# Logarithm and exponential in place of square root and reciprocal, powers on GpSimd, activation tables loaded ahead

## What is computed

```python
def _layernorm(x, axis=-1, eps=1e-05):
    m = jnp.mean(x, axis=axis, keepdims=True)
    v = jnp.var(x, axis=axis, keepdims=True)
    return (x - m) / jnp.sqrt(v + eps)

def l2norm(t):
    return t / jnp.clip(jnp.linalg.norm(t, axis=-1, keepdims=True), 1e-12)
```

## Time and profile before

| | us |
|---|---|
| Median of three runs | 2251.84 (2251.66 to 2254.59) |
| The profiled execution | 2245.9 |
| Its span in the profile | 2244.0 |
| Granted TensorE clock, mean | 0.971 |
| TensorE busy | 2001.5 |
| VectorE busy | 1459.5 |
| ScalarE busy | 1171.3 |
| GpSimd busy | 812.8 |

### The profile page before, as it was taken

One profiled execution on the slowest core, in us unless ns is written; L12 is line 12 of the kernel. 1 busy time (PEld: TensorE's weight loads), 2 busy tenths in 40 slices (PEclk: granted clock), 3 DMA queues, 4 the chain that ended last, 5 costly groups with the idle time before them and its releaser, 6 DMA issues.

```text
span 2244.0 us, 44998 instructions
## 1 busy us (share of the span) xinstructions
PE 2001.5 (89%) x17759; PEld 1185.9 (53%) x17759; DVE 1459.5 (65%) x2920; ACT 1171.3 (52%) x1950; POOL 812.8 (36%) x1153
## 2 busy tenths in 40 slices
PE   6887789988978999998998898999799899999888
PEld 3333456666644454544665444445465666666546
DVE  6775688878778777764555875121677676767474
ACT  2575456666613454565332567332576675757432
POOL 4554434333137847442001421000545344453042
PEclk9999999999989999999999999999999999999999
DMA  3430111111234424211101320000565564655161
GB/s 126 149 101 2 30 30 30 27 32 28 84 90 125 143 81 137 75 34 58 48 1 63 98 79 11 32 0 6 167 206 180 168 208 127 208 178 168 49 130 42
DMA packets 183993, 199.15 MB, mean 89 GB/s; under 512 B 55922, under 2 KB 152486, under 8 KB 179302
## 3 DMA queue, kind: packets, MB, share of 16 engines
q1 hardware_dynamic: 183782, 196.27, 29.8%
HBM read 93.53 MB, written 92.08 MB: 83 GB/s over the span
## 4 chain that ended last, share of the span: by engine, by line
PE 35%; DVE 6%; ACT 6%; issue 3%; DMA 2%; POOL 2%; SPq 1%; DVEq 0%; ACTq 0%; POOLq 0%
PE PS L2149 5%; PE PS L359 4%; PE PS L2398 3%; PE PS L2414 3%; PE PS L2386 3%; PE PS L2000 3%; ACT AR L2558 3%; PE PS L1987 2%; PE PS L1990 2%; PE PS L2752 2%; PE PS L627 1%; PE PS L2740 1%; PE PS L2742 1%; PE PS L606 1%; PE PS L2158 1%
## 5 line engine op out<-in xcount | busy, mean ns | idle before, releaser
L1314 ACT ACTIVATE AR<-PS 128x1024 f32<-128x1024 f32 x160 | 162.6, 1024 | 121.7 <-PE PS L1063 120.7
L749 ACT ACTIVATE AR<-PS 128x1024 f32<-128x1024 f32 x160 | 162.8, 1024 | 91.5 <-PE PS L606 44.9
L1167 DVE TENSOR_REDUCE AR<-PS 128x2 f32<-128x768 f32 (+1 forms) x192 | 159.9, 864 | 50.2 <-PE PS L1042 27.9
L2614 POOL TENSOR_TENSOR RA<-AR,RA 128x288 f32<-128x288 f32 x128 | 88.1, 698 | 276.8 <-DVE RA L2490 143.0
L2558 ACT ACTIVATE AR<-PS,AR 128x512 f32<-128x512 f32 x256 | 174.0, 687 | 25.6 <-DVE AR L2479 25.3
L2479 DVE TENSOR_REDUCE AR<-PS 128x2 f32<-128x1024 f32 x128 | 156.8, 1225 | 12.9
L2386 PE MATMUL PS<-AR 64*128 64x200 f32 (+2 forms) x1280 | 146.9, 354 | 3.0 <-ACT AR L2558 3.0
L1871 POOL TENSOR_TENSOR AR<-AR 128x1024 f32<-128x1024 f32 x32 | 75.5, 2358 | 173.3 <-DVE AR L1722 173.3
L2398 PEld LDWEIGHTS PS<-CC,AR 64*128 64x128 f32 x2048 | 77.9, 140 | 100.4 <-issue 78.0
L2398 PE MATMUL PS<-CC,AR 64*128 64x64 f32 x2048 | 92.4, 229 | 40.9 <-ACT AR L2542 12.4
L2386 PEld LDWEIGHTS PS<-AR 64*128 64x128 f32 x1280 | 111.1, 193 | 6.6 <-ACT AR L2558 3.2
(11 more groups left out here) (371 smaller groups left out, 5027.4 us busy)
## 6 DMA issues: line engine op xcount, KB each, us to landing
ZD<-RC SPq DMA_DIRECT2D x32, 1152.0 KB
AR<-ZD SPq DMA_DIRECT2D x32, 640.0 KB
ZP<-AR SPq DMA_DIRECT2D x128, 160.0 KB, 2.7
SP<-AR SPq DMA_DIRECT2D x40, 384.0 KB, 2.6
AR<-SP SPq DMA_DIRECT2D x128, 96.0 KB
RA<-SP SPq DMA_DIRECT2D x32, 384.0 KB
SP<-AR SPq DMA_DIRECT2D x40, 256.0 KB, 2.9
RC<-RC SPq DMA_DIRECT2D x64, 130.0 KB
```

Source lines behind the costliest of these rows:

```text
L749: e.activation(self.PT[m % 6], C.PS[:, 2 * s:2 * s + 2, :], ACT.Exp).then_inc(S["s_turned"].sem, 1)
L1167: i = e.tensor_reduce(nm[:, :, 4 * up + q:4 * up + q + 1], src[:, :, a:a + wd], AX, ALU.max, negate=True)
L1314: e.activation(self.PT[m % 6], C.PS[:, 2 * s:2 * s + 2, :], ACT.Exp).then_inc(S["s_turned"].sem, 1)
```

## The change

- Every layernorm of `Paired`, `Local`, `Shifted`, `Clipped` and `Routed`: ScalarE computes the logarithm of variance plus epsilon, waits for it on its own semaphore, and then the exponential of -0.5 times it; the reciprocal on VectorE goes, and the result is read from `ST[:, 36:40]`.
- The l2 norm of `Local`: VectorE takes the maximum with 1e-24 right behind the sums, ScalarE a logarithm and an exponential with -0.5; the reciprocal and the multiplication by 8 go from VectorE, and the 8 is in the tables `rqa` and `rqb` that the queries are multiplied with. GpSimd waits for ScalarE in place of VectorE.
- In `Experts` and `Ternary` the root goes from ScalarE to GpSimd, as a power with exponent -0.5 of 128 x 4 numbers; the exponent is a number that VectorE writes in `Begin`. "fin" becomes a step of GpSimd's and none of ScalarE's. In `Ternary` the step "gated" is called "hidden".
- Each stage has `tables`, the set that each of its kinds of steps on ScalarE needs. ScalarE preloads the first one at the start, and after each such step the next one's set if it is another. So a load stands right behind the last activation of the old set and ahead of the copies that follow it.

```diff
@@ -57,7 +57,7 @@
     tile = lambda a: a.reshape(4, 128, 64).transpose(1, 0, 2).reshape(128, 256).astype(f)
-    c["rqa"], c["rqb"], c["rka"], c["rkb"] = tile(ca * s2), tile(sa * s2), tile(ca / s2), tile(sa / s2)
+    c["rqa"], c["rqb"], c["rka"], c["rkb"] = 8 * tile(ca * s2), 8 * tile(sa * s2), tile(ca / s2), tile(sa / s2)
 
@@ -340,17 +340,23 @@
     e.tensor_scalar_add(st[:, 32:36], st[:, 25:32:2], 1e-5).then_inc(vs.sem, 1)
     w.wait_ge(ss, *key)
-    e.reciprocal(st[:, 40:44], st[:, 36:40]).then_inc(vs.sem, 1)
-    w.wait_ge(vs, *key, part=at + 4)
     for q in range(NT):
         i = e.tensor_scalar(dst[:, 128 * q:128 * q + 128], y[:, 128 * q:128 * q + 128],
-                            st[:, 24 + 2 * q:25 + 2 * q], st[:, 40 + q:41 + q], ALU.subtract, ALU.mult)
+                            st[:, 24 + 2 * q:25 + 2 * q], st[:, 36 + q:37 + q], ALU.subtract, ALU.mult)
     i.then_inc(vs.sem, 1)
 
 
 def normalise_scalar(e, w, vs, ss, key, st):
-    w.wait_ge(vs, *key, part=vs.per - 2)
-    e.activation(st[:, 36:40], st[:, 32:36], ACT.Sqrt).then_inc(ss.sem, 1)
+    w.wait_ge(vs, *key, part=vs.per - 1)
+    e.activation(st[:, 40:44], st[:, 32:36], ACT.Ln).then_inc(ss.sem, 1)
+    w.wait_ge(ss, *key, part=1)
+    e.activation(st[:, 36:40], st[:, 40:44], ACT.Exp, scale=-0.5).then_inc(ss.sem, 1)
+
+
+def normalise_gpsimd(e, C, w, vs, gs, key, st):
+    w.wait_ge(C.half)
+    w.wait_ge(vs, *key, part=vs.per - 1)
+    e.tensor_tensor(st[:, 36:40], st[:, 32:36], C.ST[:, 0, 44:45].broadcast_to((128, 4)), ALU.pow).then_inc(gs.sem, 1)
 
 
@@ -374,9 +380,13 @@
 
+EXPS, SILU, GELU, SIGM = "natural_log_exp_and_others", "silu_and_others", "gelu_and_others", "sigmoid_and_others"
+
+
 class Begin:
 
 
+    tables = {"exp": EXPS}
     head, tail, past, sent = 0, NB - 1, None, ("pad",)
@@ -386,6 +396,7 @@
         self.load = {n: C.flag("load_" + n, [()], 96 if n in ("b", "c", "rc") else 16) for n in ("x", "cc", "cb", "a", "b", "c", "rb", "rc", "rd")}
+        C.half = self.S["v_pad"]
         C.load = self.load
@@ -397,6 +408,7 @@
         if step[0] == "pad":
+            e.memset(C.ST[:, 0, 44:45], -0.5)
             e.memset(C.XT[:, :, 512:516], 0.0).then_inc(S["v_pad"].sem, 1)
@@ -427,6 +439,7 @@
 
+    tables = {"turned": EXPS, "fin": EXPS}
     FILLED = {0: {("scores", 0): 40, ("turned", 10): 11, ("turned", 25): 4, ("turned", 70): 5, ("turnx", 2): 8, ("turnx", 3): 12},
@@ -880,6 +893,7 @@
 
+    tables = {"turned": EXPS, "first": EXPS, "ln": EXPS}
     FILLED = {("turned", 40): 11, ("turned", 80): 5}
@@ -1215,11 +1229,9 @@
             w.wait_ge(S["s_ln"], b)
-            e.reciprocal(st[:, 40:44], st[:, 36:40]).then_inc(S["v_fin"].sem, 1)
-            w.wait_ge(S["v_fin"], b, part=1)
             for q in range(NT):
                 i = e.tensor_scalar(dst[:, 128 * q:128 * q + 128], y[:, 128 * q:128 * q + 128],
-                                    st[:, 24 + 2 * q:25 + 2 * q], st[:, 40 + q:41 + q], ALU.subtract, ALU.mult)
+                                    st[:, 24 + 2 * q:25 + 2 * q], st[:, 36 + q:37 + q], ALU.subtract, ALU.mult)
             i.then_inc(S["v_fin"].sem, 1)
@@ -1330,7 +1342,9 @@
             w.wait_ge(S["v_ln"], b)
-            e.activation(st[:, 36:40], st[:, 32:36], ACT.Sqrt).then_inc(S["s_ln"].sem, 1)
+            e.activation(st[:, 40:44], st[:, 32:36], ACT.Ln).then_inc(S["s_ln"].sem, 1)
+            w.wait_ge(S["s_ln"], b, part=1)
+            e.activation(st[:, 36:40], st[:, 40:44], ACT.Exp, scale=-0.5).then_inc(S["s_ln"].sem, 1)
         elif kind == "turnx":
@@ -1444,6 +1458,7 @@
 
+    tables = {"norm": EXPS, "exp": EXPS, "ln": EXPS, "fin": EXPS, "hg": GELU}
     FILLED = {("lin", 0, 0): 11, ("v", 0): 11, ("turnq", 0): 20, ("turnq", 8): 8, ("fill", 27): 10, ("fill", 31): 14, ("ot", 30): 8,
@@ -1727,13 +1742,9 @@
             L = n
-            SM, vn = self.SM[L % 3], S["v_norm"]
-            w.wait_ge(S["s_norm"], L)
-            e.tensor_scalar(SM[:, :, 0:16], SM[:, :, 0:16], 1e-12, None, ALU.max).then_inc(vn.sem, 1)
-            w.wait_ge(vn, L, part=1)
-            e.reciprocal(SM[:, :, 16:32], SM[:, :, 0:16]).then_inc(vn.sem, 1)
-            w.wait_ge(vn, L, part=2)
-            e.tensor_scalar(SM[:, :, 16:24], SM[:, :, 16:24], 8.0, None, ALU.mult).then_inc(vn.sem, 1)
+            SM = self.SM[L % 3]
+            w.wait_ge(S["v_sum"], 4 * L + 3)
+            e.tensor_scalar(SM[:, :, 0:16], SM[:, :, 0:16], 1e-24, None, ALU.max).then_inc(S["v_norm"].sem, 1)
         elif kind == "turnk":
@@ -1823,8 +1834,10 @@
             SM = self.SM[n % 3]
-            w.wait_ge(S["v_sum"], 4 * n + 3)
-            e.activation(SM[:, :, 0:16], SM[:, :, 0:16], ACT.Sqrt).then_inc(S["s_norm"].sem, 1)
+            w.wait_ge(S["v_norm"], n)
+            e.activation(SM[:, :, 0:16], SM[:, :, 0:16], ACT.Ln).then_inc(S["s_norm"].sem, 1)
+            w.wait_ge(S["s_norm"], n, part=1)
+            e.activation(SM[:, :, 16:32], SM[:, :, 0:16], ACT.Exp, scale=-0.5).then_inc(S["s_norm"].sem, 1)
         elif kind == "turnq":
@@ -1871,7 +1884,7 @@
             k3 = kq.rearrange("p (h d) -> p h d", h=16)
-            w.wait_ge(S["v_norm"], n // 4)
+            w.wait_ge(S["s_norm"], n // 4)
             w.wait_ge(S["g_sum"], n)
@@ -1921,6 +1934,7 @@
 
+    tables = {"gate2": EXPS, "hidden": SILU}
     head, tail, past, sent = 0, 0, None, ()
@@ -2069,7 +2084,7 @@
             w.wait_ge(S["v_outward"], 8 * b + 7)
-            normalise_vector(e, w, S["v_fin"], S["s_fin"], key, C.YB[:, b % 2, :], C.ST[:, b % 2, :], C.XK[:, b, :])
+            normalise_vector(e, w, S["v_fin"], S["g_fin"], key, C.YB[:, b % 2, :], C.ST[:, b % 2, :], C.XK[:, b, :])
 
@@ -2083,18 +2098,20 @@
             e.activation(self.SL[n % 3], C.bank[2 * (n % 2)], ACT.Silu).then_inc(S["s_hidden"].sem, 1)
-        elif kind == "fin":
-            b, = key
-            normalise_scalar(e, w, S["v_fin"], S["s_fin"], key, C.ST[:, b % 2, :])
         elif kind == "turnx":
             b, = key
             w.wait_ge(S["t_turnx"], b)
             e.activation(C.XT[:, b, 0:512], C.bank[7], ACT.Copy).then_inc(S["s_turnx"].sem, 1)
 
+    def on_gpsimd(self, e, w, step):
+        C, S, key = self.C, self.S, step[1:]
+        normalise_gpsimd(e, C, w, S["v_fin"], S["g_fin"], key, C.ST[:, key[0] % 2, :])
+
 
 class Ternary:
 
 
+    tables = {"hidden": SILU, "inner": GELU}
     head, tail, past, sent = 0, 0, None, ()
...
@@ -2222,6 +2241,7 @@
 
+    tables = {"exp": EXPS, "fin": EXPS}
     head, tail, past, sent = 0, 0, None, ("lay", "skew", "band", "gather", "send", "rep")
@@ -2661,6 +2681,7 @@
 
+    tables = {"gate1": SIGM, "hidden": SILU, "fin": EXPS}
     head, tail, past, sent = 0, 0, None, ("send", "rep")
@@ -3015,6 +3036,9 @@
         w = Waits(e)
+        ahead = [made[n].tables[step[0]] for what, n, step in line
+                 if what == "step" and step[0] in made[n].parts.get("s", ()) and step[0] in made[n].tables]
+        e.preload_act_table_set(ahead[0])
         for what, n, step in line:
@@ -3023,6 +3047,10 @@
                 made[n].on_scalar(e, w, step)
+                if step[0] in made[n].tables:
+                    table = ahead.pop(0)
+                    if ahead and ahead[0] != table:
+                        e.preload_act_table_set(ahead[0])
 
```

More of the change, by code:

```diff
@@ L334, in normalise_vector @@
     i.then_inc(vs.sem, 1)
-    at = vs.per - 5
+    at = vs.per - 4
     w.wait_ge(vs, *key, part=at + 1)
@@ L2109, in __init__ @@
         for pair in (0, 2):
-            self.plan += [("gated", 4 * b + c) for b in (pair, pair + 1) for c in range(4)]
+            self.plan += [("hidden", 4 * b + c) for b in (pair, pair + 1) for c in range(4)]
             if pair:
@@ L2129, in on_tensor @@
         kind, key = step[0], step[1:]
[L2130 removed]
+        if kind == "hidden":
             n, = key
```

67 lines of the change are left out of this document (34 added, 33 removed), and 4 rows, old and new, of the table cv.

## The result

| | before | after |
|---|---|---|
| Median | 2251.75 (six runs) | 2231.89 (2229.38 to 2238.07, six runs) |
| Ratio | 1 | 0.9916, interval 0.9904 to 0.9927 |
| Profiled execution | 2245.9 | 2229.4 |
| Granted clock, mean | 0.971 | 0.973 |

The kernel is 19.9 us faster by the medians, 2231.9 against a forecast of 2233 and a range of 2220 to 2246.

A forecast was written before the change was run, and what follows sets the result against it. TensorE, busy 89% of the span, bounds the kernel; other engines count only where it waits. Terms 7.4 + 2.9 + 2.6 + 1.9 + 0.5 + 1.3 + 2.0 = 18.6 us off 2245.9 give 2227.3, or 2233.2 against the median; range 2220 to 2246.

The forecast's parts named there:

- (a): First and alibi attention, four norms each: exposed table loads come off; gain 7.4 us, bounds 5 and 9.
- (b): Shifted attention: three exposed loads come off, the fourth norm pays a second activation; gain 2.9 us.
- (f): TensorE's clock: shrinking idles may end some of six slow stretches behind them; gain 2.0 us, bounds 0 and 8.
- (c): Local attention, six groups: GpSimd's multiplication starts 0.44 us earlier in each; gain 2.6 us, bounds 0 and 6.
- The half load at the end: Local attention: 0.6 us gained, half of one load, for the gelu's table loaded ahead at the stage's end.
- (d): Experts and ternary norms, moved to GpSimd: gain 5.5 - 6P, taken as 1.9 us, bounds 3.2 and -4.8.
- P: Experts and ternary norms: time from L341's end to L346's start, 0.49 us before, taken as 0.6 with GpSimd's power.
- (e): Tables loaded ahead of use elsewhere: ternary stage's first silu 0.5 us, clipped attention 1.3, routed stage 0.
- The power is slow: Rival, experts and ternary: GpSimd's power is slow; at P = 3.7 all gain is eaten, at 6 2266 us; chance 0.09.
- Hidden after all: Rival: behind the removed load something else is ready hardly earlier; gain 9.3 us, time 2243; chance 0.15.
- The loads stay: Rival: different tables still serve logarithm and exponential, so each norm pays two loads; time 2250 us; chance 0.05.

The follow-up runs named there:

- m_local: All norms of the local stage, l2 norm and layernorms, put back as before, against d_late; 2231.7 us, ratio 0.9922.
- l_clro: Norms of the clipped and routed stages put back to square root and reciprocal, against d_late; 2230.4 us, ratio 0.9910.
- d_late: The changed kernel with the same table sets, each loaded right ahead of the step that needs it; 2229.3 us, ratio 0.9905.
- j_roots: Norms of the first, alibi and shifted attention put back to square root and reciprocal, against d_late; 2238.6 us, ratio 0.9952.

## Why the prediction was right, and where not

**(a), the attentions**: right in the sum, not place by place. Forecast 7.4, the stretches give 6.3. With shorter pieces between the same products, taken where TensorE had its full clock throughout, the profiles of one form agree within 0.03, and each norm shows by itself. The first norms gained 1.19 each (forecast 1.05). The second ones were taken to be like the first and gained 0.24 each (the piece from 153.1 to 168.8 in the profile before takes 15.68 in the old form and 15.44 in the new): behind the load stood VectorE, as the wait of 0.87 above shows. The third ones gained 2.40 and 1.94 (forecast 1.7 each), more than the three idles that were added up. Two errors cancelled.

**(b), the shifted attention**: 2.9 forecast, 5.2 measured. The three waits fell by 1.2 each, 3.6. Most of the rest is what the prediction had put into (f): behind the shortened idle, the stretch that ran at 0.64 has now the full 2.4 GHz, and the products in it (817.2 to 824.0 before) take 5.88 where they took 6.80. The window of the changed kernel (us, busy times, granted clock):

```profile
810.00:818.00 8.00, 6.26 (x59) 4.12 (x60) 6.19 (x11) 4.84 (x8) 3.23 (x6) 1.00 0.22 70
```

**(c), the local stage**: right in mechanism and size, 2.6 against 3.6 by the stretches and 2.4 by m_local. GpSimd's start was what counted: 0.51 came off it and 0.49 off a whole group. So the copies behind the two activations took nothing back, though TensorE waits longer for them; the 0.6 taken off for them was not needed. The half load at the end has no run that shows it.

**(d), the experts and the ternary stage**: the term that was mis-sized. "I stay near it, with something for the longer arithmetic: P = 0.6": P is 1.12. By its own formula 5.5 - 6 x 1.12 = -1.2 in place of 1.9. The structure held (the wait passes from the silu to the norm; a second power adds 0.97 to TensorE's idle); the choice between the ends was wrong, because four elements against sixteen said nothing of a power: 128 x 16 numbers take 0.22 in the one operation, 128 x 4 take 1.02 in the other, and no row bore on the kind. The upper bound, 1.7, was in the end the nearer one (0.58 away against 0.74). The experts' last norm shows the size alone: the piece of the kernel around it takes 6.10 where it took 5.46 (two profiles of each form at the full clock), 0.64 more, and P less 0.49 is 0.63.

**(e)**: the clipped stage's 1.3 came (1.2 by the stretches, within their spread). The ternary stage's 0.5 for its first silu's table came too, as 0.66 (4.61 less 3.95), but further on the loads ahead lose 0.7. The routed stage was put at nothing and has 1.7 by the stretches; in the one profile after it was 4.7. Part of that is chance: whether small operations of VectorE meet GpSimd's. In the timeline after, a cast of 0.18 takes 0.99 and ends with GpSimd's four multiplications (2153.48 + 0.99 = 2154.47, 2149.49 + 4.94 = 2154.43):

```profile
2149.49 4.94 POOL L2890 TENSOR_TENSOR AR<-AR 128x512 f32<-128x512 f32 x4
...
2153.48 0.99 DVE L2801 CAST AR<-AR 128x32 f32<-128x32 uint32 x1
```

In the profile before three small operations close together took 0.74, 1.10 and 0.98 at another place. l_clro, with roots, costs 1.1 more than d_late, which is no more than its spread. Whether the routed stage's 1.7 belongs to the change stays open.

**(f), the clock**: 2.0 was taken, with bounds 0 and 8. Two of its slow stretches are gone, those behind the first two waits of the shifted attention: the three profiles with the old form have 3.4 us at 1.2 GHz at each, the eleven with the new form have none, and each cost 0.9. The one at the first norm stayed, 6.8 us before and after. Summed over the span, single profiles tell little (129.5 us at 1.2 GHz before, 121.2 after, 119 to 147 in the twelve experiments). The clocks of all executions tell more: their mean is 0.968 in the 51 of the kernel before that ran beside the experiments, 0.972 in the changed kernel's six, 0.971 in d_late's, 0.969 in j_roots's. Among the 51, an execution with 0.001 more clock was 1.4 us shorter. By these numbers an estimate of the clock's part is 4 to 5 us, some of it already counted in the stretches of the other terms; which of clock and time drives the other they don't show.

**The rivals.** The power is slow: right in kind, P twice what was taken, and a third of what it needed to decide. Its sign, a power under 0.5, did not come: 1.02. Hidden after all: not as a whole, 18 to 20 us came, but at the second norms of the two attentions, and there the wait passed to VectorE, which the prediction had named as a sign of being wrong. The loads stay: no, 61. The drain of 1.38 us that the Trainium skill, "ScalarE: Activation LUTs", section "What ACT_TABLE_LOAD costs", adds to a load doesn't show: removing an exposed load gave 1.18 at the first norm and 1.2 at the shifted attention's. Nor did the first power pay 6 us, as the Trainium skill, "GPSIMD Engine Reference", section "2.1 Instruction dispatch", has it for a freshly loaded routine: all eight took between 1007 and 1052 ns, and the first started 0.17 us behind L341's end, where the third started 0.08 behind it. Whether the routine was fresh there is not known.

Two figures of the working are slightly off: at P = 1.7 the sum of (d) is -4.7, not -4.8, and at 4.4 the kernel would be 4.2 slower, not 4.5. Neither moves the forecast.

That the total came within 1 us is partly luck. Against the stretches the attentions fell 1.1 short, the experts and the ternary stage 2.5 ((d) is 3.1 short by its formula), and (f)'s 2.0 has no stretch of its own; the shifted attention brought 2.3 more, the routed stage 1.7 and the local one 1.0. And the sum was made against a profiled execution that differs from its successor by 3.4 less than the medians do.

## What to carry to other kernels

Price a table load by who waits behind it: of 72 us of loads that went, a quarter was time, and most of that lay in nine norms of the attentions, where TensorE waited for ScalarE. Ask at each such place who comes next: at two of the nine it was VectorE, and 0.24 us was left of 1.2. Load a table ahead only into a real pause of the engine: ahead of a copy that TensorE waited for it cost 0.7 us in the ternary stage, in the local stage it lengthened TensorE's idle and went with more slow products, and it gained nothing measurable over a load right ahead of the step that needs it. What counts is that the load stands ahead of that step's wait and not behind it: 0.66 us at the ternary stage's first silu. A longer wait is not yet a longer time: compare the distance between the same two products. When work moves to another engine, the operation's own price there decides, and where no row shows that operation the other operations' rows bound it poorly.
